# Four buffers of exponentials, both quantisations behind a pair's second group, and values' products ahead of the next scores

## The chip, the cores and the metric

The kernel runs on one core of one Trainium2 chip. The metric is the device time of one execution in microseconds (us). TensorE is called PE in the views, its weight loads PEld, VectorE DVE, ScalarE ACT, GpSimd POOL, and SyncE with its DMA queue SP.

## What is computed

For each of 16 items of 256 tokens by 512 channels, a transformer block is computed, and then a second layer. The block is a self attention, a cross attention, and a gated feed-forward part. Both attentions have 16 heads of 32 channels, and q, k, v and the softmax weights are rounded to 8 bits. Cut to what matters here:

```python
def _fq(x, delta, zp, n_bits):
    xi = round(x / delta) + zp
    return (clip(xi, 0.0, 2.0 ** n_bits - 1.0) - zp) * delta

def _attn(x, ctx, wq, wk, wv, wo, bo, dq, dk, dv, dw):      # 16 heads of 32
    q, k, v = x @ wq, ctx @ wk, ctx @ wv
    attn = softmax(_fq(q, dq, 128., 8) @ _fq(k, dk, 128., 8).T * SCALE)
    return (_fq(attn, dw, 0., 8) @ _fq(v, dv, 128., 8)) @ wo + bo

h1 = ln(x);  x = attn(h1, h1, ...) + x        # self attention
h2 = ln(x);  x = attn(h2, ctx, ...) + x       # cross attention
h3 = ln(x);  a, g = split(h3 @ ff_w1 + ff_b1)
x = (a * gelu(g)) @ ff_w2 + ff_b2 + x
# then a cross attention of 8 heads without rounding, added to x
```

## The kernel before

Two programs run one after the other. The first, which the change is about, does both attentions of the 16 items. The second does the feed-forward part and the last attention. Every engine has an order of work written out by hand, and semaphores join them.

**Phases.** An attention of one item is a phase, of 8 groups of 2 heads by 256 tokens by 256 keys each, in quarter-tiles of 128x256. A round of the loop is two phases: the "cross" phase (`two_`, `a=1`, cross attention of item b) and the "self" phase (`one_`, `a=0`, self attention of item b+2). There is a loop of 13 rounds and one peeled round; the phases `P_A` and `P_B` stand before them and `P_Y` and `P_Z` behind. A phase is walked in 8 slots. Beside its group, each slot has "fills": projections for other items (`PHASE2_FILLS` in a cross phase, `PHASE1_FILLS` in a self phase), one half (j = 0 or 1) a slot. A fill is 12 or 24 matmuls into one of two PSUM banks `PJ`. Fills are q1, k1, v1 (self attention), q2, k2, v2 (cross), o1 and o2 (output projections), and hT and h2T (transposes of a normalised x).

**A pair of groups.** On TensorE an odd slot g begins with the scores of groups g+1 and g+2 (`pe_scores`), which fill the two score tiles `S0` and `S1` at once. So it waits until all 8 exponentials of the two groups before have been taken out of them:

```python
pe.wait_ge(exp_done, 4 * ph.group(g))
```

Then come the values' products of a pair from two pairs earlier (`pe_pv`), then the fills of slots g and g+1. I call the time from one start of scores to the next a pair, and name it by its phase and odd slot. A round is cross-1, cross-3, cross-5, cross-7, self-1, self-3, self-5, self-7. After its scores DVE takes the negated maxima of both groups (L676), POOL scales them to a bias (L773), ACT takes four exponentials of each group with their sums (L597), POOL scales the sums (L779), DVE takes the reciprocal (L684) and multiplies (`dve_probs`, L694) into `pq`, and a DMA transposes `pq` into `pT` (L897), which has four buffers.

**Tiles.** The exponentials `e` have two buffers. `act_exp` of group n waits until group n-2 has been multiplied, `act.wait_ge(prob_scaled, 4 * (n - 1))`. ACT turns a q, k or v fill into 8 bits (`act_quantise`, L564) one slot after it was filled, so one stands between a pair's two groups of exponentials and one behind them. DVE widens it (L653) two slots after. A fill's half j is in bank `PJ[j]`. The output of a half phase leaves `O` by `act_oT` (L606), ahead of the exponentials of slots 0 and 4. The transposed x (L180 and L577 on ACT, L187, L662 and L665 on DVE) has its DVE part between the two maxima of a pair. POOL adds a bias row to the next x (`pool_x_bo`, L786) in slots 0 and 1 of the self phase, the first one once the normalised x is done.

## Time and profile before

| | |
|---|---|
| median of 3 runs | 2836.47 us (2833.95 to 2840.88) |
| profiled execution, its own time | 2836.69 us |
| its span | 2834.9 us |
| self and cross attention, first to last scores | 44.6 to 1127.3 us |
| of it the loop, 12 rounds of it | 205.95 to 1003.40 us |
| second program | from 1157.9 us |
| mean granted TensorE clock | 0.971 |

The span is the profiled execution without 1.8 us around it. The busy share of an engine is a mean over stages; the change concerns the first. Times in the views are from the start of the span.

### The profile page before, as it was taken

Reading aid. Unit: us, or ns where it says so; the run is one execution under the profiler, and the core shown is the slowest. Engines: PE = TensorE matmul, PEld = TensorE weight load, DVE = VectorE, ACT = ScalarE, POOL = GpSimd, SP = SyncE. Lnnn points to the kernel's source line nnn. Section 1 sums busy time; section 2 is a strip of 40 time slices with the busy share of each in tenths; the row PEclk is TensorE's granted clock in tenths of the full one; section 3 lists DMA queues with packets and bytes.
Section 4 is the critical chain, followed back from the end, with each engine's and each line's share of the span. In section 5 each row is a group of like instructions: output and inputs, shape, how many; then the busy total and the mean of one; then the engine's idle time right before and its main releaser. Section 6 shows DMA issues by size and latency. Waiting matters only on the chain.

```text
span 2834.9 us, 54052 instructions
## 1 busy us (share of the span) xinstructions
PE 2594.9 (92%) x18304; PEld 2174.3 (77%) x18304; DVE 1652.6 (58%) x3945; ACT 1427.6 (50%) x3749; POOL 674.5 (24%) x1147
## 2 busy tenths in 40 slices
PE   5788888888888886599999999999999999999997
PEld 4566666666666664499999999999988888888885
DVE  5788888888888886454444444445344444444433
ACT  5577777777777775321111111113455555555554
POOL 1122222222222221222222222222222212212211
PEclk9899999999999997699999999999999999999999
DMA  4444433434444343512121212124011111111111
GB/s 153 88 87 85 86 85 84 94 85 91 86 85 87 83 89 60 161 68 81 52 81 52 81 52 81 52 96 149 23 52 52 44 52 52 44 44 50 53 37 38
DMA packets 335273, 211.06 MB, mean 74 GB/s; under 512 B 275568, under 2 KB 291952, under 8 KB 335216
## 3 DMA queue, kind: packets, MB, share of 16 engines
q1 hardware_dynamic: 335216, 210.34, 27.6%
q8 instruction: 31, 0.51, 0.1%
q14 instruction: 26, 0.21, 0.0%
HBM read 92.84 MB, written 50.33 MB: 51 GB/s over the span
## 4 chain that ended last, share of the span: by engine, by line
PE 55%; DVE 2%; issue 1%; ACT 1%; DMA 0%; POOL 0%; DVEq 0%; SPq 0%; POOLq 0%
PE AG L158 34%; PE Y L158 12%; PE XT L1275 2%; PE O L1298 2%; PE XT L1285 2%; PE XT L133 1%; DVE parts L1619 1%; DVE xhat L125 1%; PE Y L133 1%; PE O L1308 0%; DVE turned L187 0%; ACT stage L1515 0%; DMA stage<-in_ff_w_dram 0%; DVE mid_parts L1676 0%; POOL base L1829 0%
## 5 line engine op out<-in xcount | busy, mean ns | idle before, releaser
L158 PE MATMUL AG<-h_parts,up 128*128 128x256 f32 x6144 | 780.0, 285 | 12.0 <-DVE down L1600 8.7
L158 PEld LDWEIGHTS AG<-h_parts,up 128*128 128x128 f32 x6144 | 764.0, 193 | 24.5 <-issue 9.5
L597 ACT ACTIVATE e<-S,bias,qk_scale 128x256 f32<-128x256 f32 x1024 | 564.4, 565 | 186.8 <-POOL bias L773 135.6
L1483 ACT ACTIVATE gate<-AG,cols_pack 128x256 f32<-128x256 f32 x256 | 121.4, 474 | 672.7 <-PE AG L158 672.2
L1844 POOL TENSOR_TENSOR mid_parts<-mid_act,mid_parts 128x256 fp32r<-128x256 f32 x256 | 199.7, 780 | 1078.7 <-DVE mid_parts L1676 1078.7
L158 PE MATMUL Y<-down,mid_parts 128*128 128x512 f32 x1536 | 403.9, 400 | 0.0
L1669 DVE SCALAR_TENSOR_TENSOR mid_act<-AG,cols_pack,gate 128x256 f32<-128x256 f32 x256 | 123.4, 482 | 424.6 <-ACT gate L1483 423.8
L676 DVE TENSOR_REDUCE negmax<-S 128x4 f32<-128x1024 f32 x256 | 304.0, 1220 | 112.0 <-PE S L501 112.0
L158 PEld LDWEIGHTS Y<-down,mid_parts 128*128 128x128 f32 x1536 | 272.2, 189 | 68.8 <-issue 22.6
L694 DVE TENSOR_SCALAR pq<-e,rsum 128x256 uint16<-128x256 f32 x1024 | 306.5, 363 | 6.9 <-DMA pT<-pq 1.8
L149 PE MATMUL PJ<-w_a_wo,oT 128*128 128x512 f32 x512 | 239.1, 612 | 3.6 <-ACT oT L606 2.7
L158 PE MATMUL PJ<-hT,w_a_wq 128*128 128x256 f32 x1536 | 205.7, 293 | 22.6 <-DVE hT L665 19.5
L158 PEld LDWEIGHTS PJ<-hT,w_a_wq 128*128 128x128 f32 x1536 | 198.0, 200 | 30.9 <-issue 29.8
L597 ACT ACTIVATION_READ_ACCUMULATOR e<-S,bias,qk_scale 128x1 f32 x1024 | 209.0, 204 | 0.0
L158 PEld LDWEIGHTS AG<-parts,w_late 128*128 128x128 f32 x1536 | 190.9, 192 | 4.7 <-issue 0.8
L158 PE MATMUL AG<-parts,w_late 128*128 128x256 f32 x1536 | 192.4, 283 | 0.0
L149 PEld LDWEIGHTS PJ<-w_a_wo,oT 128*128 128x128 f32 x512 | 95.0, 195 | 108.7 <-issue 108.7
L564 ACT ACTIVATE q<-PJ,inv 128x512 int8<-128x512 f32 x192 | 132.8, 692 | 73.2 <-PE PJ L158 71.5
L773 POOL TENSOR_TENSOR bias<-negmax,qk_scale 128x4 f32<-128x4 f32 x256 | 66.3, 259 | 370.3 <-DVE negmax L676 370.3
L501 PE MATMUL S<-kT,qT 32*128 32x256 bf16 x1024 | 52.2, 278 | 110.3 <-ACT e L597 110.0
L1705 DVE TENSOR_REDUCE negmax<-XT 128x2 f32<-128x512 f32 x128 | 82.5, 686 | 104.3 <-PE XT L1275 104.3
L501 PEld LDWEIGHTS S<-kT,qT 32*128 32x128 bf16 x1024 | 15.8, 93 | 159.9 <-ACT e L597 113.1
(125 smaller groups left out, 3579.5 us busy)
## 6 DMA issues: line engine op xcount, KB each, us to landing
stage<-in_ff_w_dram SPq DMA_DIRECT2D x48, 256.0 KB, 4.8
x_in<-in_x_dram SPq DMA_DIRECT2D x16, 512.0 KB, 3.6
ctx_in<-in_ctxT_dram SPq DMA_DIRECT2D x16, 512.0 KB, 3.6
mid_dram<-x SPq DMA_DIRECT2D x16, 512.0 KB, 2.7
own<-mid_dram SPq DMA_DIRECT2D x16, 512.0 KB, 3.3
own<-in_ctx_dram SPq DMA_DIRECT2D x16, 512.0 KB, 3.5
h_dram<-h3T SPq DMA_DIRECT2D x16, 512.0 KB, 2.6
k_dram<-own SPq DMA_DIRECT2D x16, 512.0 KB, 2.6
```

What stands on the lines that cost most here:

```text
L149: last = nc.tensor.matmul(bank[:], xT[:, k, j * P:(j + 1) * P], w[:, k, :], start=(k == 0), stop=(k == KC - 1))
L158: last = nc.tensor.matmul(acc, lhs(l), rhs(r), start=(start and i == 0), stop=(stop and i == 2))
L501: ins = nc.tensor.matmul(S[i // 2][:, i % 2, qt, :], qT[ph.tiles][r:r + DH0, g // 2, qt * P:(qt + 1) * P], kT[ph.tiles][r:r + DH0, g // 2, ...
L564: nc.scalar.activation(q8[:, bank, :], PJ[bank][:], ACT.Copy, scale=inv[:, d:d + 1]).then_inc(pj_emptied[bank], 1)
L597: nc.scalar.activation(e[:, s, i, :], S[s][:, i // 2, i % 2, :], ACT.Exp, bias=bias[:, s, i:i + 1], scale=qk_scale[:, ph.a:ph.a + 1], accu ...
L676: nc.vector.tensor_reduce(negmax[:, g % 2, :], S[g % 2][:].rearrange("p i q n -> p (i q) n"), AX_X, ALU.max, negate=True).then_inc(max_don ...
L694: nc.vector.tensor_scalar(pq[:, s, i, :].bitcast(U16), e[:, s, i, :], rsum[:, s, i:i + 1], WMAX, ALU.mult, ALU.min).then_inc(prob_scaled, 1)
L773: nc.gpsimd.tensor_tensor(bias[:, g % 2, :], negmax[:, g % 2, :], qk_scale4[:, ph.a, :], ALU.mult).then_inc(bias_done, 1)
L1483: nc.scalar.activation(gate[:, f % 2, :], AG[f % 2][:, TOK:2 * TOK], ACT.Gelu, bias=ff_b1[:, c:c + 1]).then_inc(gate_done, 1)
L1669: nc.vector.scalar_tensor_tensor(out=mid_act[:, f % 2, :], in0=AG[f % 2][:, 0:TOK], scalar=ff_b1[:, c:c + 1], in1=gate[:, f % 2, :], op0=A ...
L1705: nc.vector.tensor_reduce(negmax4[:, h % 2, :], X4[h % 2], AX_X, ALU.max, negate=True).then_inc(max4_done, 1)
L1844: nc.gpsimd.tensor_tensor(mid_parts[:, f % 2, 1, :], mid_act[:, f % 2, :], mid_parts[:, f % 2, 0, :], ALU.subtract).then_inc(mid_low_done, 1)
```

## The change

Six things are moved or enlarged, all in the first program but the last.

1. `e` and the sums get four buffers in place of two, so exponentials of group n wait for the multiplication of group n-4.
2. ACT takes both quantisations of a pair behind its second group, at odd slots (`quantised_beside`); their fills are those of the two slots before. `act_oT`, the ctx copy and the transposed x stand there as well. DVE widens both at the next even slot.
3. The bank of a fill is 1-j in place of j, but for hT and h2T.
4. On TensorE `pe_pv` stands ahead of `pe_scores`.
5. DVE takes both maxima before the transposed x. `pool_x_bo` is moved to slot 7 of the cross phase and slot 1 of the self phase, both gated by `pool_beside_max`; the load of x moves behind the transpose of slot 1.
6. `P_Y` has its k2 fills in slot 4 and v2 in 6 and 7. The rows `ff_b2` and `bv` are loaded at the start of the second program, no longer at the start of the first.

```diff
         PAIR_BUFS = 4
+        E_BUFS = 4
 
         def bank_of(stage, name, j):
 
-            return 1 - j if name == "q2" and stage == "last" else j
+            return j if name.split("@")[0] in ("hT", "h2T") else 1 - j
...
                 for g in range(GROUPS):
                     if g % 2:
+                        if g >= 5:
+                            pe_pv(pe, ph, g - 5)
+                        elif prev:
+                            pe_pv(pe, prev, g + GROUPS - 5)
                         if g + 1 < GROUPS:
                             pe_scores(pe, ph, g + 1)
                         elif nxt:
                             pe_scores(pe, nxt, 0)
-                        if g >= 5:
-                            pe_pv(pe, ph, g - 5)
-                        elif prev:
-                            pe_pv(pe, prev, g + GROUPS - 5)
...
-                if not (isinstance(n, int) and n < 2):
-
-                    act.wait_ge(prob_scaled, 4 * (n - 1))
+                if not (isinstance(n, int) and n < E_BUFS):
+
+                    act.wait_ge(prob_scaled, 4 * (n - E_BUFS + 1))
...
+            def quantised_beside(ph, prev, g):
+
+                if early(ph) and g == 6:
+                    return late(ph, prev, 5)
+                if early(ph) and g == 7:
+                    return late(ph, prev, 6)
+                return late(ph, prev, g - 2, g - 1) if g % 2 else []
+
+            def widened_beside(ph, prev, g):
+                if early(ph) and g == 7:
+                    return late(ph, prev, 5)
+                if g == 0 and prev and early(prev):
+                    return late(ph, prev, -2)
+                return late(ph, prev, g - 3, g - 2) if g % 2 == 0 else []
...
-                    if prev and g in (0, 4):
-                        act_oT(act, prev, g // 4)
                     act_exp(act, ph, g)
-                    for where in late(ph, prev, g):
+                    for where in quantised_beside(ph, prev, g):
                         if kind_of(where[2]) in QUANTISED:
                             act_quantise(act, where)
                     for where in transposed(ph, g, 0):
                         act_transposed(act, where)
-                    if g == ph.ctx_at:
+                    if g == 1 and prev and prev.a == 0:
+                        act_oT(act, prev, 0)
+                    if g == 3 and prev:
+                        act_oT(act, prev, 1)
+                    if g == 7 and ph.a == 1:
+                        act_oT(act, ph, 0)
+                    if ph.ctx_at is not None and g == ph.ctx_at - 1:
                         act_ctx_high(act, ph, prev)
...
                     if g % 2 and into:
-                        dve_max(dve, into, m)
+                        for i in range(2):
+                            dve_max(dve, into, m + i)
                     for where in transposed(ph, g, 1):
                         dve_transposed(dve, where)
-                    if g % 2 and into:
-                        dve_max(dve, into, m + 1)
...
-                    if g in (0, 1) and ph.a == 0 and ph.stage in ("loop", "peeled"):
-
-                        if g == 0:
-                            pool.wait_ge(ln["xhat_done"], TT * (ln_x1(ph.b + 1) + 1))
-                        else:
-                            pool_beside_max(pool, ph, g)
-                        pool_x_bo(pool, ph.b + 2, g)
+                    if ph.stage in ("loop", "peeled") and (ph.a, g) in ((1, 7), (0, 1)):
+                        half = 1 - ph.a
+                        wait_emptied(pool, (ph.stage, ph.b, "o1", half))
+                        pool_beside_max(pool, ph, g)
+                        pool_x_bo(pool, ph.b + 2, half)
```

On TensorE, in the loop from the second fill of cross-1 to the first of cross-3 (S are scores, O the values' products, PJ a fill), the order before is:

```order
L158 MATMUL PJ<-hT,w_a_wk 128x256 x24
L494 REGISTER_ALU
L497 ISA
L501 MATMUL S<-kT,qT 128x256 x8
L526 MATMUL O<-pT,vQ 32x256 x8
L158 MATMUL PJ<-hT,w_a_wk 128x256 x24
```

And of the changed kernel at the same place:

```order
L156 MATMUL PJ<-hT,w_a_wk 128x256 x24
L524 MATMUL O<-pT,vQ 32x256 x8
L492 REGISTER_ALU
L495 ISA
L499 MATMUL S<-kT,qT 128x256 x8
L156 MATMUL PJ<-hT,w_a_wk 128x256 x24
```

The products have changed places with the scores and their wait. On ACT, from slot 0 of the cross phase to slot 1 (e are exponentials, q a quantised fill, oT the output of a half phase), the order before is:

```order
L606 ACTIVATE oT<-O,wv_scale 128x512
L592 ISA
L595 ISA
L597 ACTIVATE e,sums<-S,bias,qk_scale 128x256 x4
L433 REGISTER_ALU
L562 ISA
L564 ACTIVATE q<-PJ,inv 128x512
L592 REGISTER_ALU
L595 REGISTER_ALU
L597 ACTIVATE e,sums<-S,bias,qk_scale 128x256 x4
L433 ISA
L562 ISA
```

And of the changed kernel:

```order
L594 ACTIVATE e,sums<-S,bias,qk_scale 128x256 x4
L589 REGISTER_ALU
L592 ISA
L594 ACTIVATE e,sums<-S,bias,qk_scale 128x256 x4
L431 ISA
L560 ISA
L562 ACTIVATE q<-PJ,inv 128x512
L431 ISA
L560 ISA
L562 ACTIVATE q<-PJ,inv 128x512
L599 ISA
L603 ACTIVATE oT<-O,wv_scale 128x512
```

The output and the quantisation no longer stand ahead of or between the two groups of exponentials, but behind them. On DVE, in slot 7 of the self phase (negmax are the maxima), the order before is:

```order
L676 TENSOR_REDUCE negmax<-S 128x4
L433 REGISTER_ALU
L187 TENSOR_SCALAR turned<-PJ,cols_pack 128x256 x2
L662 CAST hT<-turned 128x512
L664 ISA
L665 TENSOR_TENSOR hT<-turned,hT 128x1024
L675 REGISTER_ALU
L676 TENSOR_REDUCE negmax<-S 128x4
```

And of the changed kernel:

```order
L696 TENSOR_REDUCE negmax<-S 128x4
L695 REGISTER_ALU
L696 TENSOR_REDUCE negmax<-S 128x4
L431 REGISTER_ALU
L185 TENSOR_SCALAR turned<-PJ,cols_pack 128x256 x2
L682 CAST hT<-turned 128x512
L684 ISA
L685 TENSOR_TENSOR hT<-turned,hT 128x1024
```

The second maximum has moved ahead of the transposed x.

## Rows read from the trace of the kernel before

**Rows 1.** The page: busy time, share of the span, instructions of each engine.

```profile
PE 2594.9 (92%) x18304; PEld 2174.3 (77%) x18304; DVE 1652.6 (58%) x3945; ACT 1427.6 (50%) x3749; POOL 674.5 (24%) x1147
```

**Rows 2.** Windows: stretch, its length, busy time PE, PEld, DVE, ACT, POOL, clock, DMA.

```profile
205.95:1003.40 797.45, 704.20 (x4993) 514.57 (x4993) 669.90 (x1632) 598.57 (x1813) 190.83 (x493) 0.97 0.41 87
539.79:605.17 65.38, 57.35 (x416) 41.64 (x416) 55.77 (x136) 49.87 (x152) 15.89 (x42) 1.00 0.41 88
```

**Rows 3.** Timeline of PE, one round: start, length, instructions, idle before and its releaser.

```profile
530.24 0.40 PE L501 MATMUL S<-kT,qT 32*128 32x256 bf16 x8 [0.76 <-ACT e L597]
...
539.79 0.40 PE L501 MATMUL S<-kT,qT 32*128 32x256 bf16 x8 [0.81 <-ACT e L597]
...
546.96 0.40 PE L501 MATMUL S<-kT,qT 32*128 32x256 bf16 x8 [0.49 <-ACT e L597]
...
554.64 0.40 PE L501 MATMUL S<-kT,qT 32*128 32x256 bf16 x8 [0.44 <-ACT e L597]
...
561.75 0.40 PE L501 MATMUL S<-kT,qT 32*128 32x256 bf16 x8
...
570.95 0.40 PE L501 MATMUL S<-kT,qT 32*128 32x256 bf16 x8 [2.66 <-ACT e L597]
...
576.77 3.04 PE L158 MATMUL PJ<-hT,w_a_wq 128*128 128x256 f32 x24
580.50 0.40 PE L501 MATMUL S<-kT,qT 32*128 32x256 bf16 x8 [0.69 <-ACT e L597]
...
587.67 0.40 PE L501 MATMUL S<-kT,qT 32*128 32x256 bf16 x8
...
595.62 0.40 PE L501 MATMUL S<-kT,qT 32*128 32x256 bf16 x8 [0.76 <-ACT e L597]
```

**Rows 4.** Waits in 205.95 to 1003.40: total, times, longest.

```profile
ACT e L597 <- POOL bias L773: 95.5, 72, 2.1
...
PE S L501 <- ACT e L597: 67.5, 71, 2.7
...
ACT e L597 <- DVE pq L694: 43.5, 54, 1.3
```

**Rows 5.** Timeline of all engines in cross-1: maxima, exponentials, quantisation.

```profile
540.22 2.36 DVE L676 TENSOR_REDUCE negmax<-S 128x4 f32<-128x1024 f32 x2 [1.36 <-PE S L501]
...
541.84 0.56 ACT L597 ACTIVATE e<-S,bias,qk_scale 128x256 f32<-128x256 f32 x1 [1.53 <-POOL bias L773]
...
544.02 0.69 ACT L564 ACTIVATE q<-PJ,inv 128x512 int8<-128x512 f32 x1
```

**Rows 6.** DMA issues in 205.95 to 1003.40: count, median us to landing.

```profile
pT<-pq SPq DMA_TRANSPOSE x192, 3.0
```

**Rows 7.** Timeline of DVE, from cross-5 into cross-7.

```profile
555.07 2.36 DVE L676 TENSOR_REDUCE negmax<-S 128x4 f32<-128x1024 f32 x2 [0.51 <-PE S L501]
...
562.81 2.35 DVE L676 TENSOR_REDUCE negmax<-S 128x4 f32<-128x1024 f32 x2
```

**Rows 8.** Timeline of all engines in cross-7: multiplications beside POOL's row addition.

```profile
566.24 1.38 POOL L786 TENSOR_TENSOR x_bo<-x_in,rows 128x512 f32<-128x512 f32 x1 [1.94 <-DVE xhat L125]
566.39 2.18 DVE L694 TENSOR_SCALAR pq<-e,rsum 128x256 uint16<-128x256 f32 x4
...
568.88 1.13 DVE L694 TENSOR_SCALAR pq<-e,rsum 128x256 uint16<-128x256 f32 x4
```

**Rows 9.** Timeline of all engines in self-1: the transposed x on DVE.

```profile
507.37 0.99 DVE L187 TENSOR_SCALAR turned<-PJ,cols_pack 128x256 f32<-128x256 f32 x2
...
510.07 1.22 DVE L676 TENSOR_REDUCE negmax<-S 128x4 f32<-128x1024 f32 x1
```

**Rows 10.** Windows (columns as in 2): self-1 in two other rounds.

```profile
834.46:845.99 11.53, 10.26 (x72) 9.22 (x73) 8.02 (x18) 7.28 (x22) 1.40 (x5) 0.70 0.42 95
...
901.81:911.36 9.55, 7.77 (x72) 6.90 (x72) 7.91 (x18) 7.38 (x22) 1.40 (x5) 1.00 0.49 108
```

**Rows 11.** Timeline of all engines at the start: the v weights' second halves.

```profile
17.71 3.52 DVE L424 TENSOR_TENSOR w_a_wv<-x,w_a_wv 128x512 fp32r<-128x512 f32 x4 [4.71 <-ACT w_a_wv L419]
```

**Rows 12.** Windows (columns as in 2): phases P_A and P_B; the last phases.

```profile
44.59:129.02 84.43, 56.23 (x366) 43.97 (x365) 62.04 (x140) 54.36 (x161) 13.88 (x39) 0.82 0.44 94
...
1066.35:1109.27 42.92, 32.79 (x208) 24.57 (x209) 27.48 (x67) 25.05 (x75) 8.26 (x22) 0.86 0.27 50
```

More of the change, by code:

```diff
@@ L73, in build @@
         bq_scaled = sb(ctx, "bq_scaled", [P, KC])
-        rows2 = sb(ctx, "rows2", [P, 2, D])
-        rows = {n: rows2[:, i] for i, n in enumerate(ROWS2)}
+        rows = {}
         deltas = sb(ctx, "deltas", [P, 8])
@@ L275, in __init__ @@
                 self.tiles = a if tiles is None else tiles
-                self.ctx_at = {id(PHASE2_FILLS): 4, id(P_A_FILLS): 4, id(P_Y_FILLS): 0}.get(id(fills))
+                self.ctx_at = {id(PHASE2_FILLS): 4, id(P_A_FILLS): 4, id(P_Y_FILLS): 2}.get(id(fills))
                 self.ctx_seq = 0 if stage == "first" else b + 1
@@ L357, in build @@
             q8 = sb(one, "q8", [P, 2, D], I8)
-            e = sb(one, "e", [P, 2, 4, TOK])
+            e = sb(one, "e", [P, E_BUFS, 4, TOK])
             pq = sb(one, "pq", [P, 2, 4, TOK], F16)
@@ L607, in act_oT, with late, early @@
                                      scale=wv_scale[:, ph.a:ph.a + 1]).then_inc(oT_done, 1)
-            def late(ph, prev, g, by=1):
-                p, s = (ph, g - by) if g >= by else (prev, g + GROUPS - by)
-                if p is None:
-                    return []
-                return [at(p.stage, p.b, n, j) for n, j in p.steps(s) if kind_of(n) not in ("hT", "h2T")]
+            def late(ph, prev, *slots):
+                found = []
+                for g in slots:
+                    p = ph if g >= 0 else prev
+                    if p is not None:
+                        found += [at(p.stage, p.b, n, j) for n, j in p.steps(g % GROUPS)]
+                return found
+            def early(ph):
+                return ph is P_B or ph is P_Y
+            def quantised_beside(ph, prev, g):
[10 more added lines that the diff above has]
+                return late(ph, prev, g - 3, g - 2) if g % 2 == 0 else []
             def transposed(ph, g, j):
@@ L632, in act_phase @@
                         act_transposed(act, where)
-                    if g == ph.ctx_at:
+                    if g == 1 and prev and prev.a == 0:
[5 more added lines that the diff above has]
+                    if ph.ctx_at is not None and g == ph.ctx_at - 1:
                         act_ctx_high(act, ph, prev)
             def act_drain(act, ph):
-                for half in range(2):
-                    act_oT(act, ph, half)
+                act_oT(act, ph, 1)
             def tiles_of(stage, name):
@@ L725, in dve_phase @@
                             dve_weight_low(dve, c)
-                    fills = [f for f in late(ph, prev, g, 2) if kind_of(f[2]) in QUANTISED]
+                    fills = [f for f in widened_beside(ph, prev, g) if kind_of(f[2]) in QUANTISED]
                     if g:
@@ L732, in dve_phase @@
                     if g % 2 and into:
-                        dve_max(dve, into, m)
+                        for i in range(2):
+                            dve_max(dve, into, m + i)
                     for where in transposed(ph, g, 1):
                         dve_transposed(dve, where)
-                    if g % 2 and into:
-                        dve_max(dve, into, m + 1)
                     if g == ph.ctx_at:
                         dve_ctx(dve, ph, prev)
-                    for where in late(ph, prev, g):
-                        if kind_of(where[2]) not in QUANTISED:
+                    for where in late(ph, prev, g - 1):
+                        if kind_of(where[2]) in ("o1", "o2"):
                             dve_residual(dve, where)
@@ L1086, in build @@
             stage_down = stage[:, 2, :].rearrange("p (s d) -> p s d", s=2)
+            rows2 = sb(both_halves, "rows2", [P, 2, D])
+            rows.update({n: rows2[:, i] for i, n in enumerate(ROWS2)})
             base = sb(both_halves, "base", [P, TT, D])
```

36 lines of the change are left out of this document (19 added, 17 removed).

## The prediction

> **What bounds the kernel now.** I read the page first: TensorE is busy 92% of the span, DVE 58%, ACT 50% [rows 1]. That is a mean over two programs, and the change is in the first, so I went to windows. Twelve rounds of the loop take 797.45 us, 66.45 each, with DVE busy 84%, ACT 75%, TensorE 88%. One round at full clock takes 65.38, TensorE 57.35 of it [rows 2]. So TensorE is the fullest engine there but idle for 8 us a round, and the question is what ends that idle time.
>
> The timeline of TensorE shows it [rows 3]. The reader is to see nine starts of scores, and in brackets how long TensorE sat idle before each and for whom. The pairs last 7.17 (cross-1), 7.68 (cross-3), 7.11 (cross-5), 9.20 (cross-7), 9.55 (self-1), 7.17 (self-3), 7.95 (self-5) and 9.55 (self-7). The idle times at their ends are 0.49, 0.44, none, 2.66, 0.69, none, 0.76 and 0.81. The releaser is always the last exponential. The view of waits says what holds the exponentials: the bias 72 times, 95.5 us, and the multiplication of the group two before 54 times, 43.5 us [rows 4].
>
> One pair in close-up [rows 5]: scores start at 539.79 [rows 3], the first exponential at 541.84, so 2.05 for maximum and bias. Four exponentials take 2.18, to 544.02. Then a quantisation of 0.69 stands in the way, then four more exponentials, and the next scores start at 546.96. That is 2.05 + 2 x 2.18 = 6.41, and 0.76 for the quantisation and handovers. Of the 0.76 I take 0.2 as handover.
>
> **What the change removes, piece by piece.** I lay out one round anew from these lengths.
>
> *Exponentials.* Without quantisation between the groups and without the wait for the multiplication, the chain from scores to scores is 6.41 + 0.2 = 6.6. TensorE's own work in a pair is the pair less its idle time: cross-1 6.68, cross-3 7.24, cross-5 7.11, cross-7 6.54, self-3 7.17, self-5 7.19. All but one are over 6.6, so TensorE becomes the bound where nothing else is late. The two quantisations go behind the exponentials, 1.4 us, into the 2.05 in which ACT waits for the next bias. In cross-3 an output copy and a ctx copy, 0.69 and 0.63 long as such ACT operations are (0.69 in [rows 5]), make it 2.7, so exponentials start 0.6 late; TensorE's 7.24 hides it. Removed: 0.49 in cross-1, 0.44 in cross-3, 0.76 in self-5.
>
> *The swapped banks.* The first fill of a pair now needs the bank whose quantisation follows the exponentials: ready 6.6 + 0.7 = 7.3 after the scores before, though TensorE wants it two products (0.66) after its own scores. Where a pair lasts 6.7 that is at 7.36: no wait. Bounds: nothing, and 0.7 a pair. I take nothing, as the exponentials then run ahead of TensorE.
>
> *Values' products ahead.* They are the same 0.33 of work in another place. They cost nothing while the transposed probabilities have landed. The second group's multiplication ends about 4.6 into the following pair, the DMA takes 3.0 [rows 6], and the products are due three pairs after the scores, near 21: some 5 us of slack.
>
> *DVE.* It is the next engine. From the maxima of cross-5 to those of cross-7 it has 7.74 of unbroken work (555.07 to 562.81), against 7.11 of TensorE [rows 3, 7]. In the changed kernel a widening is added there (about 0.3), so 8.0: the maxima of cross-7 are 0.9 late. There POOL's row addition (1.38 in [rows 8]) now stands ahead of the bias and costs another 0.4. Cross-7 becomes 6.6 + 0.9 + 0.4 - 0.2 (slack) = 7.7, down from 9.20: it loses the wait of 2.66.
>
> *The port.* In cross-7 four multiplications took 2.18 beside POOL's addition and 1.13 alone [rows 8]. The addition is moved beside the maxima, so DVE gets back 1.05 a round. The Trainium skill, "SBUF — State Buffer", "Who interferes with whom", says that DVE and GpSimd share a pair of ports as an exclusive lock, which a DVE tensor_scalar takes and a reduction never does. By that rule, the trace agrees, the move gives the whole 1.05, and by the row too; it lies in what cross-7 loses, not beside it.
>
> *The transposed x.* In self-1 and self-7 DVE's part (507.37 to 510.07, 2.70 [rows 9]) now comes behind both maxima, 1.2 later. It ends 0.43 + 2.28 + 2.70 = 5.4 after the scores (0.43 from 539.79 to 540.22 [rows 3, 5]; 2.28 as two maxima end before their 2.36 are up). The second fill waits for it. That fill starts at 576.77 now, 5.82 after the scores of 570.95 [rows 3], so it isn't later than before: about 5.7. Then 3.0 for the fill and 0.33 for the products: 9.05. In self-7 DVE arrives 0.1 late, 9.15. So 0.5 and 0.4 are won.
>
> Sum of a round: 6.7 + 7.2 + 7.1 + 7.7 + 9.05 + 7.2 + 7.15 + 9.15 = 61.25, against 65.38. DVE would be busy 55.77 - 1.05 = 54.7 of it, 89%, so it has little room. I take 61.5 for handovers that the sum leaves out. 14 rounds (13 and the peeled one): 14 x 3.9 = 54.
>
> *Clock.* The mean round is 66.45, not 65.38 [rows 2]; the excess of 12 rounds is 12.9. It comes as one kind of event: self-1 takes 11.53 at a granted clock of 0.70 where it takes 9.55 at 1.00 [rows 10], partly at 1.2 GHz in place of 2.4, always after cross-7 with its idle 2.66. With that down to 1.2 most should go, though self-1 keeps its own idle time. Bounds: none gone, 15 gone (14 rounds). I take 10. The Trainium skill, "TensorE: Matmul & The Clock Gate", "Terms", prices such a stretch at half its cold time. By that a cold stretch of 6.9, which is what a mean clock of 0.70 over 11.53 comes to, costs 3.5; the rows say 2.0, since part of it is idle time anyway, and I use the rows.
>
> *Outside the loop.* At the start two 256 KB row loads leave the queue ahead of the v weights, which DVE awaited for 4.71 and then split in 3.52 [rows 11]: 2 won, bounds 0 and 3. P_A and P_B take 84.43 with TensorE busy 56.23 [rows 12]. ACT and DVE split weights there, so little is hidden anew: 2 won, bounds -3 and 8. P_Y is 42.92 long [rows 12]; its k2 fills (6 us) leave slots 1 and 2, where they were not hidden by 2.4, and stand beside the normalisation in slot 4, but v2 moves into the long pair: nothing, bounds -3 and 3. The row loads in the second program are issued while its queue waits for a free weight buffer: nothing.
>
> Total: 54 + 10 + 2 + 2 = 68. Against the profiled execution's own 2836.69 (span 2834.9 and 1.8 around it), which is within 0.3 of the median 2836.47, that is 2768.
>
> **Rivals.**
> - *DVE becomes the bound, half the gain.* For: it is busy 54.7 of 61.5, has 8.0 of work in cross-5 against 7.11, and every late maximum delays bias, exponentials and scores. Against: self-3 and cross-1 have slack in which it catches up. If each phase loses 0.9 more, a round is 63.3: 14 x 2.1 = 29, with half of the clock's 15 and 2: 2798.
> - *Fills wait for the quantisation.* If exponentials end only when TensorE is ready, each first fill starts 0.5 late, 8 x 0.5 = 4 a round, which eats the gain: a round of 65.5, with only the clock's 10 and 2: 2826. For it speaks that both quantisations are now late in the order; against it that exponentials run ahead in long pairs.
> - *Slower: products block the scores.* TensorE takes its order as written. If the transposed probabilities land after it reaches the products, the scores behind them wait too, which they did not before. It decides from the point where DVE's second multiplication is over 5 us later than in my layout. 1 us of wait a pair is 8 a round; 61.5 + 8 = 69.5, 14 x 4.1 = 57 lost: 2894. Against it: the slack.
> - *No change.* The bound is the bias chain, and what exponentials lose in one wait they get in another; the 95.5 of bias waits [rows 4] are larger than the 43.5. Then 2834. Against: in cross-7 the wait of 2.66 is plainly for a multiplication.
>
> **How the numbers follow.** The forecast 0.62 (its own range 2752 to 2786), half gain 0.20, quantisation 0.06, slower 0.06, no change 0.06. This kernel's measurement tells 0.3%, 8.5 us. Faster: 0.62 + 0.20 + 0.06 = 0.88; same 0.06; slower 0.06. The range reaches to the half gain's case and a little over: 2750 to 2804; it leaves out the last three cases (0.18). The lower end is all of the clock's 15, the 61.25 and 7 more outside the loop.
>
> **What would show it.** Rounds of 61 to 62; cross-7 near 7.7 with an idle time of about 1.2 before self-1; no wait of exponentials for the multiplication; multiplications of 1.1 in cross-7; scores waiting for exponentials in cross-7 alone; fills of self-1 and self-7 waiting for the transposed x; no self-1 of 11.5, or few. Wrong would be: TensorE's products waiting for a DMA, fills waiting for the quantisation in plain pairs, or DVE maxima over 1 us behind the scores in most pairs.

## The result and the profile after

The changed kernel takes 2758.85 us (median of 4 runs, 2754.95 to 2764.56), the kernel before in the same series 2837.56 (4 runs, 2833.95 to 2840.88). The ratio is 0.9724, with a 95% interval of 0.9703 to 0.9746: faster. The forecast was 2768 with a range of 2750 to 2804. The profiled execution took 2758.9, its span is 2757.1 and its mean clock 0.978, against 2834.9 and 0.971.

The page of the changed kernel, busy time of the engines, to be laid beside [rows 1]:

```profile
PE 2578.8 (94%) x18304; PEld 2157.8 (78%) x18304; DVE 1640.1 (59%) x3945; ACT 1416.1 (51%) x3749; POOL 680.9 (25%) x1147
```

Counts are the same and the busy times nearly: nothing was saved in work, it was moved. Windows of the changed kernel, columns as in [rows 2]: twelve rounds, one round at full clock, one self-1 at a lower clock, and P_A with P_B up to its slot 7:

```profile
193.18:929.96 736.78, 692.53 (x4996) 502.43 (x4993) 658.90 (x1632) 588.91 (x1813) 196.32 (x493) 0.99 0.44 94
499.94:561.14 61.20, 57.42 (x422) 41.59 (x419) 54.91 (x136) 49.07 (x152) 16.32 (x42) 1.00 0.44 94
466.91:476.65 9.74, 9.12 (x73) 8.10 (x74) 7.94 (x18) 7.85 (x23) 2.08 (x6) 0.82 0.35 65
42.66:123.09 80.43, 54.73 (x374) 43.24 (x374) 62.38 (x140) 54.19 (x161) 14.40 (x39) 0.83 0.47 99
```

A round went from 66.45 to 736.78 / 12 = 61.40, one at full clock from 65.38 to 61.20, with the same 57.4 of TensorE's work in it. TensorE is now idle for 3.8 a round where it was for 8.0. The timeline of TensorE in that round, as [rows 3]:

```profile
499.94 0.40 PE L499 MATMUL S<-kT,qT 32*128 32x256 bf16 x8
...
506.55 0.40 PE L499 MATMUL S<-kT,qT 32*128 32x256 bf16 x8
507.11 3.14 PE L156 MATMUL PJ<-hT,w_a_wk 128*128 128x256 f32 x24 [0.17 <-ACT q L562]
...
513.96 0.40 PE L499 MATMUL S<-kT,qT 32*128 32x256 bf16 x8
...
520.99 0.40 PE L499 MATMUL S<-kT,qT 32*128 32x256 bf16 x8
...
528.88 0.40 PE L499 MATMUL S<-kT,qT 32*128 32x256 bf16 x8 [1.34 <-ACT e L594]
529.55 1.13 PE L131 MATMUL PJ<-ident,xhat 128*128 128x128 f32 x8 [0.28 <-ACT q L562]
531.40 3.14 PE L156 MATMUL PJ<-ctxT,w_a_wk 128*128 128x256 f32 x24 [0.71 <-ACT turned L178]
...
537.81 0.40 PE L499 MATMUL S<-kT,qT 32*128 32x256 bf16 x8
...
557.73 3.14 PE L156 MATMUL PJ<-hT,w_a_wq 128*128 128x256 f32 x24 [0.52 <-DVE hT L685]
560.80 0.40 PE L524 MATMUL O<-pT,vQ 128*32 128x256 f16 x8
561.13 0.40 PE L499 MATMUL S<-kT,qT 32*128 32x256 bf16 x8
```

Scores wait for exponentials in one pair of eight, cross-7, and for 1.34 in place of 2.66. The other brackets are new or were small: fills that wait for a quantisation or the transposed x. Waits of the changed kernel in 193.18 to 929.96 (total, times, longest), as [rows 4]:

```profile
ACT e L594 <- POOL bias L793: 102.1, 60, 2.3
...
PE PJ L156 <- ACT turned L178: 16.5, 24, 0.8
...
PE S L499 <- ACT e L594: 16.1, 12, 1.3
...
PE PJ L156 <- DVE hT L685: 6.3, 12, 0.6
```

Exponentials' wait for the multiplication, 43.5 before, is gone from the list, and scores wait 16.1 in place of 67.5. The largest row shown, ACT waiting for the bias, grew from 95.5 to 102.1 while the kernel became faster: in most pairs this is a wait of an engine ahead of TensorE's need.

The span shrank by 77.8. From the starts of scores in the timeline: the first scores start 1.9 earlier; P_A and P_B take 4.0 less (84.43 to 80.43); the 14 rounds take 70.9 less; the rest about 1.

The eight pairs, median of 13 rounds, in the order cross-1, 3, 5, 7, self-1, 3, 5, 7. In the last column is the sum, and in brackets the mean round. Where most rounds of a pair ran at a lowered clock, its median holds that too (self-1 of five kernels with 9.7 and more, self-7 of `u_two_buffers` and `o_products_ahead`). All the kernels run are in it; the first row and the second were on record before the run:

| kernel | pairs | sum (mean) |
|---|---|---|
| before, full clock | 7.17 7.68 7.11 9.20 9.55 7.17 7.95 9.55 | 65.38 (66.5) |
| changed, as forecast | 6.7 7.2 7.1 7.7 9.05 7.2 7.15 9.15 | 61.25 |
| changed, measured | 6.61 7.41 7.04 7.89 8.94 7.17 7.04 9.12 | 61.22 (61.4) |
| changed, run again | 6.61 7.39 7.04 7.88 8.94 7.17 7.04 9.12 | 61.2 (61.9) |
| `u_two_buffers` | 6.96 7.42 7.22 8.24 9.66 7.41 8.13 9.88 | 64.9 (65.0) |
| `u_quantise_between` | 7.17 7.17 7.04 8.28 8.94 7.17 7.04 8.93 | 61.7 (62.0) |
| `u_bank_j` | 6.61 7.41 7.04 7.89 12.21 7.17 7.04 10.08 | 65.4 (65.8) |
| `u_products_behind` | 6.61 7.17 7.04 7.89 8.60 7.17 7.04 8.78 | 60.3 (60.3) |
| `u_turned_between` | 6.86 7.17 7.04 7.89 9.75 7.17 7.04 8.59 | 61.5 (61.4) |
| `u_row_add_old` | 6.61 7.41 7.04 8.80 10.29 7.17 7.04 9.12 | 63.5 (63.5) |
| `o_four_buffers` | 7.17 7.69 7.13 8.52 11.51 7.17 7.13 9.28 | 65.6 (64.7) |
| `o_products_ahead` | 7.17 7.68 7.04 9.26 11.65 7.17 7.95 10.33 | 68.2 (67.9) |
| `o_rows_only` | 7.17 7.68 7.11 9.19 9.56 7.17 7.94 9.55 | 65.4 (66.1) |
| `next_version` | 6.86 7.17 7.04 7.47 8.93 7.17 7.04 8.60 | 60.3 (60.5) |
| `products_behind_bias_first` | 6.61 7.17 7.04 7.47 8.60 7.17 7.04 8.78 | 59.9 (59.9) |

### The profile page after: what moved, and what is told of

The parts are those of the page before. It is cut to its first block, busy times and chain, and to the rows that moved or that the text cites. A ratio compares the mean times of both kernels' runs of the same rounds, so it can differ in the third digit from the quotient of the medians.

```text
span 2757.1 us, 54077 instructions
## 1 busy us (share of the span) xinstructions
PE 2578.8 (94%) x18304; PEld 2157.8 (78%) x18304; DVE 1640.1 (59%) x3945; ACT 1416.1 (51%) x3749; POOL 680.9 (25%) x1147
## 4 chain that ended last, share of the span: by engine, by line
PE 56%; DVE 2%; issue 1%; ACT 1%; DMA 0%; POOL 0%; DVEq 0%; SPq 0%; POOLq 0%
PE AG L156 35%; PE Y L156 13%; PE XT L1295 3%; PE O L1318 2%; PE XT L1305 2%; PE XT L131 1%; DVE parts L1639 1%; DVE xhat L123 1%; PE Y L131 1%; PE O L1328 0%; DVE turned L185 0%; ACT stage L1535 0%; DMA stage<-in_ff_w_dram 0%; DVE mid_parts L1696 0%; ACT stage L1544 0%
## 5 line engine op out<-in xcount | busy, mean ns | idle before, releaser
L714 DVE TENSOR_SCALAR pq<-e,rsum 128x256 uint16<-128x256 f32 x1024 | 292.4, 349 | 13.7 <-DMA pT<-pq 1.2
L594 ACT ACTIVATION_READ_ACCUMULATOR e<-S,bias,qk_scale 128x1 f32 x1024 | 215.2, 210 | 0.0
L799 POOL TENSOR_TENSOR dsum<-sums,delta_w 128x4 f32<-128x4 f32 x256 | 70.4, 275 | 279.3 <-ACT e L594 279.3
L1696 DVE CAST mid_parts<-mid_act 128x256 fp32r<-128x256 f32 x256 | 84.4, 330 | 86.6 <-PE Y L156 82.3
```

The lines of the kernel that those rows point to most:

```text
L594: nc.scalar.activation(e[:, g % E_BUFS, i, :], S[g % 2][:, i // 2, i % 2, :], ACT.Exp, bias=bias[:, g % 2, i:i + 1], scale=qk_scale[:, ph. ...
L714: nc.vector.tensor_scalar(pq[:, s, i, :].bitcast(U16), e[:, g % E_BUFS, i, :], rsum[:, s, i:i + 1], WMAX, ALU.mult, ALU.min).then_inc(prob ...
L1696: nc.vector.tensor_copy(mid_parts[:, f % 2, 0, :], mid_act[:, f % 2, :]).then_inc(mid_high_done, 1)
```

## The experiments

The kernels named `u_` are the changed kernel with one part undone, those named `o_` the kernel before with one part done. Ratios are to the kernel before, with 95% intervals. The changed kernel stands at 0.9724. Not undone by themselves are the new places of `act_oT` and the ctx copy, and P_Y's fills.

**Two buffers again.** The rest of the change stays.

```diff
-        E_BUFS = 4
+        E_BUFS = 2
```

> The changed kernel with two buffers of exponentials again, all else kept. My layout of a round: the second group's exponentials must then wait for the multiplication that stands behind both maxima (and behind the transposed x in self-1 and self-7). That ends 4.6 us after the scores in a plain pair (needed at 4.25), 7.3 in self-1, 6.9 in self-7, 6.1 in cross-7, 5.8 in self-5, so pairs lengthen by 0.8 (self-1), 0.3 (self-7), 0.6 (cross-7), 1.1 (self-5), 0.3 (cross-1), 0.2 (cross-5): 3.3 a round, rounds of 64.5, some 46 us over the changed kernel, ratio to before about 0.989. Rival, the buffers are the change and the rest only ornament: all of the gain is given back, ratio 1.00, or more than that as the maxima now stand together. Rival, the buffers are not what counts, the quantisation is: under 10 us lost, ratio 0.975.

Measured: 2810.03, ratio 0.9909 [0.9893, 0.9926]. Its waits from 190 to 900, the two largest of exponentials:

```profile
ACT e L594 <- DVE pq L714: 77.0, 88, 2.0
...
ACT e L594 <- POOL bias L793: 76.7, 54, 2.1
```

The wait for the multiplication is back, and larger than the 43.5 of [rows 4]. It costs 3.2 a round at full clock, where self-7 takes 9.33: each pair is off its expected loss by 0.3 at most. The clock is lowered in three self-1 and in seven self-7, which then take 9.9. P_A and P_B are 4.9 longer than in the changed kernel. Without the buffers two thirds of the gain are gone.

**A quantisation between the groups again.** Quantising after every slot, widening two slots after the fill.

```diff
-                return late(ph, prev, g - 2, g - 1) if g % 2 else []
+                return late(ph, prev, g - 1)
...
-                return late(ph, prev, g - 3, g - 2) if g % 2 == 0 else []
+                return late(ph, prev, g - 2)
```

> The changed kernel with each quantisation one slot behind its fill and the widening two, as before: one stands between the two groups of exponentials again. My layout: the chain from scores to scores is 7.17 again where a fill of the even slot's predecessor is a q, k or v (cross-1, cross-3, cross-7, self-3, self-7), which counts where TensorE is not the longer: cross-1 +0.55, cross-7 +0.6, cross-3 +0.1, self-1 0 to -0.3 (its transposed x starts earlier on ACT). About 1.0 a round, 14 us, ratio 0.977. Rival, the quantisation out of the chain is the main part: 0.6 in each pair, 60 us, ratio 0.993.

Measured: 2775.65, 0.9794 [0.9778, 0.9811]. Cross-1 is 7.17 again, cross-7 0.39 longer, but cross-3 0.24 shorter: there the first fill no longer waits 0.17. Self-7 is 0.19 shorter. A round is 0.5 longer, not 1.0 as expected. P_A and P_B up to slot 7 take 3.6 more than in the changed kernel. That need not be this part's share of the 4.0 won there: with two buffers again they take 4.9 more, while the products ahead alone, on the kernel before, take 3.0 off them. What each part is worth there was not separated.

**Banks as they were.**

```diff
-            return j if name.split("@")[0] in ("hT", "h2T") else 1 - j
+            return j
```

> The changed kernel with every fill's half j in bank j again. My layout: only self-1 and self-7 notice: the first fill behind the transposes then needs the bank that DVE empties, 3.85 us after the scores, in place of ACT's at 2.2 to 2.5, so that the second fill starts at 6.8 in place of 5.6 to 5.7: 1.2 + 1.1 = 2.3 a round, 32 us, ratio 0.983. Rival, the swap of banks is neutral because the second fill waits for DVE's subtraction anyway (it did in self-7, by 0.52): under 0.7 a round, under 10 us, ratio 0.975.

Measured: 2822.19, 0.9956 [0.9941, 0.997]. Self-7 is 0.96 longer, as expected within 0.2. In four rounds it is at a lowered clock as well. Self-1 takes 11.5 to 12.4 in all 13 rounds. TensorE there, and the window of that pair:

```profile
555.38 0.40 PE L499 MATMUL S<-kT,qT 32*128 32x256 bf16 x8 [1.35 <-ACT e L594]
556.63 1.96 PE L131 MATMUL PJ<-ident,xhat 128*128 128x128 f32 x8 [0.86 <-ACT q L562]
...
559.68 4.63 PE L156 MATMUL PJ<-ctxT,w_a_wk 128*128 128x256 f32 x24 [1.09 <-DVE turned L185]
```

```profile
555.38:567.46 12.08, 10.13 (x73) 9.11 (x75) 8.02 (x18) 7.96 (x23) 2.43 (x6) 0.72 0.42 94
```

The transposes wait 0.86 for the second quantisation in place of 0.28 for the first, and the fill behind them 1.09 for DVE's part. The same 8 transposes take 1.96 instead of 1.13 and the 24 matmuls 4.63 instead of 3.14, at a granted clock of 0.72. The two added waits, 0.96 together, cost 3.1 in this pair (12.08 against 8.94), the larger part by the clock. The prediction had priced the swap of banks by what waits for the quantisation in plain pairs; its value lies in self-1.

**Products behind the scores again.**

```diff
+                        if g + 1 < GROUPS:
+                            pe_scores(pe, ph, g + 1)
...
                         if g >= 5:
                             pe_pv(pe, ph, g - 5)
                         elif prev:
                             pe_pv(pe, prev, g + GROUPS - 5)
-                        if g + 1 < GROUPS:
-                            pe_scores(pe, ph, g + 1)
```

> The changed kernel with the values' products behind the next pair's scores again. My layout: the same 0.33 of TensorE work in another place; where TensorE is the bound nothing changes, and only cross-7, whose end is idle, may lose 0.3: rounds of 61.2 to 61.6, 0 to 5 us, ratio 0.972 to 0.975. Rival, the swap fills TensorE's idle time at the end of each pair: 0.33 x 8 x 14 = 37 us lost, ratio 0.986.

Measured: 2745.79, 0.9684 [0.9668, 0.970]. By the medians that is 13 us faster than the changed kernel, by the ratios and by the spans of the profiled executions (2746.2 against 2757.1) 11. Both numbers expected were too high. TensorE around self-1:

```profile
523.59 0.40 PE L499 MATMUL S<-kT,qT 32*128 32x256 bf16 x8 [1.34 <-ACT e L594]
523.92 0.40 PE L524 MATMUL O<-pT,vQ 128*32 128x256 f16 x8
524.27 1.14 PE L131 MATMUL PJ<-ident,xhat 128*128 128x128 f32 x8
526.12 3.13 PE L156 MATMUL PJ<-ctxT,w_a_wk 128*128 128x256 f32 x24 [0.71 <-ACT turned L178]
529.14 3.13 PE L156 MATMUL PJ<-hT,w_a_wq 128*128 128x256 f32 x24
532.20 0.40 PE L499 MATMUL S<-kT,qT 32*128 32x256 bf16 x8
```

The products fill the 0.28 in which TensorE otherwise waits for the bank, and the next scores follow straight upon the second fill: 8.60 for the pair. Ahead of the scores they stand behind that second fill, and the pair is 0.34 longer, in self-7 as well; cross-3 loses 0.24. Of 13 rounds none has a self-1 at a lowered clock, against 3 in the changed kernel. At the end the order is worth something: P_Y and P_Z from their first scores to their last take 71.65 here and 68.28 in the changed kernel, 3.4 that the products ahead gain there. P_A and P_B are 1.3 longer here as well.

**The transposed x between the maxima again.**

```diff
                     if g % 2 and into:
-                        for i in range(2):
-                            dve_max(dve, into, m + i)
+                        dve_max(dve, into, m)
                     for where in transposed(ph, g, 1):
                         dve_transposed(dve, where)
+                    if g % 2 and into:
+                        dve_max(dve, into, m + 1)
```

> The changed kernel with DVE's part of the transposed x between the two maxima again. My layout: in self-7 DVE is what the second fill waits for (0.52 idle), so self-7 gains 0.4 to 0.5 if the second maximum, 2.7 later, does not make the exponentials end after TensorE (they would end at about 8.5 of 8.6); self-1, where TensorE itself is the longer, stays at 8.94 or loses 0.1. Rounds of 60.8, 6 us faster than the changed kernel, ratio 0.970. Rival, the order of the maxima is what keeps the exponentials in time: self-1 and self-7 each lose 0.5 to 1, rounds of 62.5, ratio 0.979.

Measured: 2756.36, 0.9718 [0.9703, 0.9733], no difference to the changed kernel. Inside it two things cancel: self-7 is 0.53 shorter, and self-1 takes 9.75 in place of 8.94 in 12 rounds of 13. (Cross-3 is 0.24 shorter and cross-1 0.25 longer besides.) In one of the 12 (526.86 to 536.65) the mean clock is 0.83. In the one round without that, self-1 takes 8.80. TensorE in that round, and in the one at 0.83:

```profile
404.69 0.40 PE L499 MATMUL S<-kT,qT 32*128 32x256 bf16 x8 [1.34 <-ACT e L594]
405.36 1.14 PE L131 MATMUL PJ<-ident,xhat 128*128 128x128 f32 x8 [0.28 <-ACT q L562]
407.21 3.14 PE L156 MATMUL PJ<-ctxT,w_a_wk 128*128 128x256 f32 x24 [0.71 <-ACT turned L178]
...
526.86 0.40 PE L499 MATMUL S<-kT,qT 32*128 32x256 bf16 x8 [1.34 <-ACT e L594]
527.53 1.43 PE L131 MATMUL PJ<-ident,xhat 128*128 128x128 f32 x8 [0.28 <-ACT q L562]
529.38 4.13 PE L156 MATMUL PJ<-ctxT,w_a_wk 128*128 128x256 f32 x24 [0.41 <-ACT turned L178]
```

The transposes are already slow, 1.43 in place of 1.14, before the last wait, which then is shorter. So the clock fell before that wait, and the wait of 0.41 did not cause the fall. This part of the change costs self-7 0.53, and it is the clock that pays it back.

**The row addition in its old slots.** `pool_x_bo` in slots 0 and 1 of the self phase, as the removed lines of the diff have it.

```diff
-                    if ph.stage in ("loop", "peeled") and (ph.a, g) in ((1, 7), (0, 1)):
...
+                    if g in (0, 1) and ph.a == 0 and ph.stage in ("loop", "peeled"):
```

> The changed kernel with POOL's row addition in slots 0 and 1 of the self phase again, the first behind the normalised x. My layout: the four multiplications of cross-7 take 2.2 again in place of 1.14, and the second bias waits behind the addition until about 5.8 after the scores, so the exponentials end at 8.5 in place of 7.9: 0.6 a round, 8 us, ratio 0.975. Rival, port and place are nothing since DVE has slack there: rounds of 61.2 as before, ratio 0.972; or even faster by the 0.4 that the addition ahead of the bias costs, 60.8.

Measured: 2786.76, 0.9831 [0.9816, 0.9846]. All engines in cross-7 of this kernel:

```profile
535.97 1.38 POOL L806 TENSOR_TENSOR x_bo<-x_in,rows 128x512 f32<-128x512 f32 x1 [1.94 <-DVE xhat L123]
536.11 2.17 DVE L714 TENSOR_SCALAR pq<-e,rsum 128x256 uint16<-128x256 f32 x4
...
537.31 0.25 POOL L793 TENSOR_TENSOR bias<-negmax,qk_scale 128x4 f32<-128x4 f32 x1
...
537.67 0.56 ACT L594 ACTIVATE e<-S,bias,qk_scale 128x256 f32<-128x256 f32 x1 [1.22 <-POOL bias L793]
...
540.02 0.40 PE L499 MATMUL S<-kT,qT 32*128 32x256 bf16 x8 [2.26 <-ACT e L594]
```

The addition stands ahead of the second group's bias and makes four multiplications take 2.17, as in [rows 8]. Only the first of the two is on the path: with four buffers the second group's exponentials wait 1.22 for the bias, while the multiplications are still running (536.11 to 538.28). Cross-7 is 8.80, 0.91 longer, with 2.26 idle before the scores, and self-1 is at a lowered clock in all 13 rounds (9.7 to 11.2). Of the 28 us, 14 x 0.9 = 13 are cross-7, and the rest lies in self-1. No round of it ran at full clock, so how much of that rest is the clock was not separated.

**Four buffers alone** on the kernel before. The two rows leave the first program as in the change, since the tile needs their room.

```diff
+        E_BUFS = 4
...
-                    act.wait_ge(prob_scaled, 4 * (n - 1))
+                    act.wait_ge(prob_scaled, 4 * (n - E_BUFS + 1))
```

> The kernel before with four buffers of exponentials and sums alone (and the late load of ff_b2 and bv, which makes room for them). My layout: the waits for the multiplication go (3.6 us of exponentials' idle time a round), of which the path gets back 0.7 in self-5, 0.7 in cross-7 (the second bias still waits behind the row addition), 0.4 in self-1 and 0.5 in self-7: 2.3 a round, 32 us, and 7 for clock and start: ratio 0.986. Rival, the buffers are the change: 70 us, ratio 0.975. Rival, the wait goes over to the bias: under 8 us, ratio 0.997.

Measured: 2808.19, 0.9903 [0.9888, 0.9918]. Cross-7 loses 0.7 and self-5 0.8; self-1 takes 9.03 or 11.5, the latter in 9 of 14 rounds. At full clock the round would be 63.1 (the medians, with 9.04 for self-1), 2.3 less than before, which is what the layout said; with the clock it is 64.7.

**The rows alone**, loaded in the second program.

```diff
-            for i, n in enumerate(ROWS2):
-                sp.dma_start(rows2[:, i], t[n].partition_broadcast(P)).then_inc(consts_loaded, 16)
```

> The kernel before with only the loads of ff_b2 and bv moved to the start of the second program. My layout: the first scores start 2.3 us earlier (44.6 to 42.3), nothing is lost later: ratio 0.9992. Rival, the loads now delay the second program's weights: 2 us lost there, ratio 1.000.

Measured: 2833.70, 0.9991 [0.9982, 1.0001]: as expected, though the interval allows nothing as well. The first scores start at 42.15 in place of 44.60, but P_A and P_B take 86.55 in place of 84.42, so most of the start's gain is given back there in this execution.

**Products ahead alone** on the kernel before.

```diff
-                        if g + 1 < GROUPS:
-                            pe_scores(pe, ph, g + 1)
...
+                        if g + 1 < GROUPS:
+                            pe_scores(pe, ph, g + 1)
```

> The kernel before with the values' products ahead of the scores alone. My layout: where the exponentials end a pair, the products lie in TensorE's idle time but the next scores start at the same time; only in self-1 and self-7 do the transposes behind the scores start 0.33 earlier and the exponentials behind them too: 0.3 x 2 x 14 = 8 us, ratio 0.997. Rival, the swap shortens each of the six pairs that end idle by 0.33: 28 us, ratio 0.990. Rival, products wait at the head of the order for their transposes: slower than before.

Measured: 2852.66, 1.0064 [1.0048, 1.0079]: slower. Windows of its self-7 and of the self-1 in the loop, columns as before:

```profile
529.91:540.27 10.36, 9.00 (x60) 7.33 (x61) 8.01 (x18) 7.96 (x23) 1.69 (x5) 0.84 0.43 107
571.43:583.08 11.65, 10.28 (x72) 9.42 (x73) 8.01 (x18) 7.38 (x22) 1.60 (x6) 0.71 0.41 94
```

Self-1 is at 0.71 in 12 of 13 rounds, where the kernel before has it so in 7, and self-7 takes 10.3 to 10.4 from the fifth round on. Against the kernel before, the 13 self-1 take 11.3 more together and nine self-7 some 0.8 more each, 18 in all, where the 14 rounds take 20 more: what this kernel loses lies there, at the lowered clock.

**The changed kernel again**, for the scatter of its clock.

> The changed kernel itself, beside the version with the two further moves on the same chip: rounds of 61.22, ratio 0.972.

Measured: 2758.67, 0.9725 [0.9712, 0.9739]. The pairs are the same to 0.02, but six self-1 lie over 9.5, two of them at 11.4 and 11.5. Against a full clock 9.2 are lost so, where the other profiled execution lost 2.4. How often the clock falls differs from run to run, which is some 6 us between the two profiled executions.

**A next version**: self-7 alone has its transposed x between the maxima, and in cross-7 the row addition comes behind the first bias.

```diff
+                        if not (ph.a == 0 and g == 7):
+                            dve_max(dve, into, m + 1)
...
-                    if ph.stage in ("loop", "peeled") and (ph.a, g) in ((1, 7), (0, 1)):
+                    if ph.stage in ("loop", "peeled") and (ph.a, g) == (0, 1):
...
                         pool_bias(pool, nxt, 0)
+                    if ph.stage in ("loop", "peeled") and (ph.a, g) == (1, 7):
...
+                        pool_x_bo(pool, ph.b + 2, 0)
```

> The changed kernel with two further moves: in slot 7 of the self phase (and of the early phases) DVE's transposed x stands between the maxima, and POOL's row addition in cross-7 stands behind the first bias, not ahead of it. My layout: self-7 9.12 to 8.6, cross-7 7.89 to 7.45, self-1 unchanged: rounds of 60.3, 13 us faster than the changed kernel, ratio to before 0.968. Rival, DVE is full (54.7 us of a round of 61.2), so what is saved in one pair comes back in the next: rounds of 61.2, ratio 0.972.

Measured: 2749.07, 0.9699 [0.9682, 0.9715]. That is 10 us under the changed kernel in the same series, where 13 were expected. Cross-7 loses 0.42, self-7 0.52 and cross-3 0.24, cross-1 gets 0.25 longer. Three self-1 of 13 are at a lowered clock (10.1).

**Products behind and bias first**: products ahead in P_Y and P_Z alone, the row addition as in the next version, the maxima as in the changed kernel.

```diff
+                        ahead = ph is P_Y or ph is P_Z
+                        if not ahead:
...
+                                pe_scores(pe, ph, g + 1)
...
+                        if ahead:
```

> The changed kernel with the products behind the scores (but for the last two phases, where ahead was 3.4 us the better), and POOL's row addition of cross-7 behind the first bias. If the prices measured apart add up: self-7 8.78, cross-3 7.17, self-1 8.60 as with the products behind, cross-7 7.47 as with the bias first, rounds of 59.87, no stretch at half clock in the loop: 1.35 a round under the changed kernel's 61.22, 19 us, 2 for the clock, so 2738, ratio 0.965. Rival, DVE is full, so the 0.42 of cross-7 comes back in self-1: rounds of 60.3, 2744, ratio 0.9675.

Measured: 2737.88 (2736.54 to 2738.64), 0.9648 [0.9635, 0.9661], 21 us faster than the changed kernel and the fastest of all. POOL in its cross-7, and its round:

```profile
514.49 0.20 POOL L800 TENSOR_TENSOR bias<-negmax,qk_scale 128x4 f32<-128x4 f32 x1 [1.15 <-DVE negmax L703]
514.74 1.29 POOL L813 TENSOR_TENSOR x_bo<-x_in,rows 128x512 f32<-128x512 f32 x1
515.99 0.38 POOL L800 TENSOR_TENSOR bias<-negmax,qk_scale 128x4 f32<-128x4 f32 x1
```

```profile
482.29:542.15 59.86, 57.28 (x418) 41.56 (x419) 55.13 (x137) 49.16 (x151) 16.04 (x41) 1.00 0.46 96
```

The first bias is out before the addition, so the exponentials start 0.4 earlier. That 0.42 does not come back in self-1, which stays at 8.60. DVE is busy 55.13 of 59.86 and no pair got longer by it, and the 13 rounds have no half clock at all.

## Why the prediction was right, point by point

The time was 9 us under the forecast and inside its own range (2752 to 2786). Its mechanism was in the main the one that ran, and the layout of a round by hand, 61.25, met 61.22. That the two sums meet so closely is in part luck: cross-3 and cross-7 took 0.4 more together than was said, the other six 0.43 less. The forecast itself had allowed 61.5.

**Exponentials: right.** 6.7 was said for cross-1, it is 6.61; self-5 lost 0.9 of its 7.95. The wait for the multiplication is gone, also with the buffers alone. Their worth depends on the rest: 3.2 a round when taken out of the changed kernel, and 2.3 when put alone into the kernel before. That gave 28 us and not 32, as self-1 goes on falling to the lower clock (8 of 13 rounds).

**The swapped banks: wrong in its reason, small in the sum.** The step said that TensorE wants the bank "two products (0.66)" after its scores. With products ahead only the scores (0.33) stand between, so in cross-3 the fill waits 0.17, and the pair is 7.41 instead of 7.2. The larger thing was overlooked: without the swap, 63 us are lost in self-1 and self-7.

**"They cost nothing" of the values' products: wrong.** That was the step that failed. No wait for a DMA appeared, as was said. But a block of 0.33 was treated as the same work wherever it stands, and it isn't: in self-1 and self-7 the second fill is released by a chain (transposes, ACT's and DVE's part of the transposed x), so whatever stands behind that fill lengthens the pair, and whatever stands ahead of it lies in idle time. Undone, it gives 0.34 + 0.34 + 0.24 = 0.92 a round, 13 us over 14 rounds, and 2.4 of half-clock stretches besides; against it stand 3.4 in P_Y and P_Z and 1.3 in P_A and P_B, which leaves the 11 between the profiled executions.

**DVE in cross-7: right, 0.2 short.** The timeline of all engines in cross-7 of the changed kernel:

```profile
522.31 2.35 DVE L696 TENSOR_REDUCE negmax<-S 128x4 f32<-128x1024 f32 x2
522.63 1.29 POOL L806 TENSOR_TENSOR x_bo<-x_in,rows 128x512 f32<-128x512 f32 x1 [0.45 <-DVE pq L714]
...
524.03 0.20 POOL L793 TENSOR_TENSOR bias<-negmax,qk_scale 128x4 f32<-128x4 f32 x1
524.34 0.57 ACT L594 ACTIVATE e<-S,bias,qk_scale 128x256 f32<-128x256 f32 x1 [2.23 <-POOL bias L793]
...
525.88 1.14 DVE L714 TENSOR_SCALAR pq<-e,rsum 128x256 uint16<-128x256 f32 x4
```

The maxima start 522.31 - 520.99 = 1.32 after the scores, 0.9 later than the 0.43 of a free pair: that is the step's 0.9. The addition then ends at 523.92, some 0.4 after the first maximum: that is its 0.4. What it deducted as slack, 0.2, wasn't there: 6.6 + 0.9 + 0.4 = 7.9, measured 7.89. Two later kernels put the addition behind the bias, and both have 7.47, 0.42 less; the other moves in them leave cross-7 at 7.89 where they were made without it (`u_products_behind`, `u_turned_between`).

**The port: right in size, not on the path.** Four multiplications take 1.14 here in place of 2.18 [rows 8], and 2.17 again with the addition put back. The reductions beside the addition take 2.35, no more than the 2.36 of [rows 5]. That is the rule of the Trainium skill, "SBUF — State Buffer", "Who interferes with whom", which the forecast used, in both its halves. But the forecast put the 1.05 into what cross-7 loses, and there it does not lie: with four buffers no exponential waits for the multiplication. What the old place of the addition costs cross-7, 0.91, is its delay of the second group's bias.

**The transposed x: right.** 9.05 and 9.15 were said for self-1 and self-7, 8.94 and 9.12 measured. For self-7 the old order would have been better by 0.53: the gain there came from elsewhere, and the move of the maxima took part of it.

**Clock: 12 instead of 10, in part luck.** The kernel before loses 14.8 in 13 rounds to self-1 at a lowered clock, the changed one 2.4 in its profiled run. Run again it loses 9.2, which would leave 6. The forecast gave as the reason the shorter idle time before self-1; `u_row_add_old`, with 2.26, and `u_turned_between`, with the changed kernel's own 1.34, fell in 13 and in 12 rounds, so that idle time alone does not decide.

**Outside the loop: 4.0 instead of 2** for P_A and P_B; 1.9 for the start where 2 was said. P_Y and P_Z gained 0.4 (68.65 to 68.28) where nothing was said, which holds a loss and the 3.4 of the products ahead. The sum: 14 x 4.16 = 58 instead of 54, 12 instead of 10, 4 instead of 2, and 2.

**The rivals.** DVE as the bound: its work reached 90% of a round (54.91 of 61.20), and what it delayed is cross-7 by 0.9 and the second fill of self-7 by 0.52; the last kernel puts it at 92% without a loss. Fills waiting for the quantisation: 0.17 in one pair of eight, 0.28 in self-1. Products that block the scores: no wait of theirs for a DMA in any kernel. On that side of the question, though, products ahead alone do make the kernel slower, by 0.64%, for a reason that no rival named: the clock. No change: the 95.5 of bias waits grew to 102.1 and did not matter. This rival was answered with cross-7, whose wait of 2.66 "is plainly for a multiplication". That is a quarter of it: with four buffers alone cross-7 loses 0.67, and the second bias still stands behind the row addition.

## What to carry to other kernels

Before moving an independent block on an in-order engine, find the instruction in each stretch that is released by a chain: ahead of it the block can lie in idle time and cost nothing, behind it it cost its whole length here (0.34 for 0.33), so the same move can gain in one phase and lose in another. Price a part in the company that it will have: four buffers were worth 28 us alone and 51 among the others (2.3 and 3.2 a round at full clock). And a sum of waits tells nothing until one knows whether its engine is ahead of the one that sets the end, as the bias waits show.

## What the hardware showed that was not expected

Most half clock of the loop falls in self-1, and its idle times alone do not say how often. This is TensorE's idle time before the scores, then between scores, transposes and fill (in a round at full clock where the kernel has one), and in how many of 13 rounds the granted clock was lowered in self-1. Each count is from one profiled execution:

| kernel | before | behind | rounds |
|---|---|---|---|
| `products_behind_bias_first` | 0.93 | 0.71 | 0 |
| `u_products_behind` | 1.34 | 0.71 | 0 |
| `next_version` | 0.93 | 0.28 + 0.71 | 3 |
| changed, and again | 1.34 | 0.28 + 0.71 | 3, and 6 |
| `u_turned_between` | 1.34 | 0.28 + 0.71 | 12 |
| `u_two_buffers` | 1.69 | 0.28 + 0.71 | 3, and self-7 in 7 |
| `u_quantise_between` | 1.73 | 0.76 | 5 |
| `o_four_buffers` | 1.98 | 1.09 | 8 |
| before, and `o_rows_only` | 2.65 | 1.09 | 7, and 5 |
| `u_bank_j` | 1.35 | 0.86 + 1.09 | 13, and self-7 in 4 |
| `u_row_add_old` | 2.26 | 0.28 + 0.34 to 0.71 | 13 |
| `o_products_ahead` | 2.73 | 0.28 + 1.09 | 13, and self-7 in 9 |

Between the second and the fourth row the only difference is where 0.33 of products stand, and the mean clock of the whole execution bears it out in every run: 0.979 to 0.981 in four of `u_products_behind`, 0.974 to 0.978 in nine of the changed kernel. But the changed kernel and `u_turned_between` have the same idle times there, and the clock is lowered in 3 or 6 rounds of the one and in 12 of the other. A fall to 1.2 GHz costs the pair 0.8 at a mean clock of 0.82, 2.0 at 0.70; in `u_bank_j` 0.96 of added waits came back as 3.1. The table is an observation of thirteen rounds a kernel. Which of the idle times the chip reacts to was not separated, and why the clock of the same order differs from round to round stays open.

The Trainium skill, "TensorE: Matmul & The Clock Gate", "HAM oscillation — how this bites in real kernels", has half clock come from long waits for a DMA. Here TensorE waits for no DMA before self-1 and no single idle time of a loop is over 2.73, and yet `u_bank_j` has half clock in all 13 self-1. In the round shown TensorE is idle for 1.35 and for 0.86 with eight score matmuls between; the transposes behind that are slow already (1.96), before the wait of 1.09. Its remedy, an order of work that keeps TensorE busy between waits, agrees with the runs: with the products in the idle 0.28 there was no such stretch in 26 rounds of two kernels.
